# Local attention in an fp32 Trainium2 block: P divided before it is turned, and V as the stationary operand

## What is computed

```python
qkv = x @ Wqkv
q, k, v = jnp.split(qkv, 3, -1)              # then by heads: b, h, n, d
q = l2norm(q) * qs;  k = l2norm(k) * ksc
q = q * cos * scale + rotate_half(q) * sin * scale
k = k * cos * inv + rotate_half(k) * sin * inv
...
sim = jnp.einsum('bhwie,bhwje->bhwij', bq, bk2) * QK_SCALE   # 32 queries, 64 keys
sim = jnp.where(mask, -jnp.finfo(sim.dtype).max, sim)
attn = jax.nn.softmax(sim, -1)
out = jnp.einsum('bhwij,bhwje->bhwie', attn, bv2)
return out.transpose(0, 2, 1, 3).reshape(b, n, INNER) @ Wo
...
xn = (x - mu) / jnp.sqrt(var + 1e-05) * g + bln
hg = xn @ W1 + b1
a, gate = jnp.split(hg, 2, -1)
return a * jax.nn.gelu(gate, approximate=False) @ W2 + b2
```

## Time and profile before

| | us |
|---|---|
| median of three runs | 1783.48 (1780.46 to 1783.8) |
| profiled execution | 1771.68 |
| its span, first to last instruction | 1769.9 |
| TensorE busy in it | 1633.4 (92%) |
| VectorE, ScalarE, GpSimd busy | 1340.1, 1292.9, 1061.1 |

### The profile page before, as it was taken

How to read it: one execution, slowest core, us unless ns; L and a number is a source line. 1 busy time by engine, 2 the same in 40 slices (tenths; PEclk the granted TensorE clock), 3 DMA queues, 4 the chain that set the end, 5 groups by cost and what they waited for, 6 DMA issues and landing times.

```text
span 1769.9 us, 88661 instructions
## 1 busy us (share of the span) xinstructions
PE 1633.4 (92%) x36636; PEld 1264.3 (71%) x36636; DVE 1340.1 (76%) x1952; ACT 1292.9 (73%) x2124; POOL 1061.1 (60%) x767
## 2 busy tenths in 40 slices
PE   4898677799999999999999999999999999999985
PEld 2466455677777777777777777777777777777764
DVE  4465666688888878888887888888887878888852
ACT  3687445677877778777788777878777787777763
POOL 4000345567866767867678766668676676767630
PEclk8899889999999999999999999999999999999997
DMA  2000142222242222333222422222422222222220
GB/s 95 1 1 0 25 116 59 52 70 66 67 128 59 67 59 69 103 88 74 53 69 59 128 66 71 69 52 65 122 69 71 66 67 70 70 67 69 66 47 25
DMA packets 75302, 116.88 MB, mean 66 GB/s; under 512 B 17246, under 2 KB 26716, under 8 KB 74332
## 3 DMA queue, kind: packets, MB, share of 16 engines
q1 hardware_dynamic: 75228, 115.99, 26.4%
HBM read 19.04 MB, written 1.05 MB: 11 GB/s over the span
## 4 chain that ended last, share of the span: by engine, by line
PE 87%; issue 6%; ACT 4%; DVE 3%; DMA 0%; POOL 0%; ACTq 0%; SPq 0%; DVEq 0%
PE ps L684 14%; PE ps L788 10%; PE ps L671 9%; PE ps L766 9%; PE ps L731 8%; PE ps L675 7%; PE ps L674 7%; PE ps L834 4%; PE ps L724 2%; PE ps L806 2%; PE ps L808 2%; PE ps L807 2%; PE ps L801 2%; PE ps L795 2%; PE ps L582 1%
## 5 line engine op out<-in xcount | busy, mean ns | idle before, releaser
L411 POOL TENSOR_TENSOR arena<-arena,rnorm 128x1024 f32<-128x1024 f32 x192 | 361.6, 1904 | 352.3 <-ACT rnorm L1030 352.3
L402 POOL TENSOR_TENSOR arena<-arena 128x1024 f32<-128x1024 f32 x192 | 456.6, 2378 | 18.5 <-DVE arena L1349 15.1
L684 PEld LDWEIGHTS ps<-cst,arena 64*128 64x128 f32 x6144 | 224.4, 140 | 127.8 <-issue 119.0
L1345 DVE TENSOR_TENSOR arena<-ps,rope 128x1024 f32<-128x1024 f32 x192 | 234.7, 1222 | 94.9 <-issue 82.1
L684 PE MATMUL ps<-cst,arena 64*128 64x64 f32 x6144 | 276.8, 231 | 17.0 <-ACT arena L1060 9.4
L1066 ACT ACTIVATE arena<-ps 128x512 f32<-128x512 f32 x192 | 114.6, 597 | 175.5 <-PE ps L684 175.2
L1349 DVE TENSOR_TENSOR arena<-ps,rope 128x1024 f32<-128x1024 f32 x192 | 233.2, 1215 | 0.0
L674 PE MATMUL ps<-wqkv_lo,x_hi 128*128 128x512 f32 x576 | 229.2, 398 | 1.1 <-issue 1.1
L675 PE MATMUL ps<-wqkv_hi,x_hi 128*128 128x512 f32 x576 | 230.1, 399 | 0.0
L671 PE MATMUL ps<-wqkv_hi,x_lo 128*128 128x512 f32 x576 | 216.2, 457 | 14.8 <-issue 12.9
L1359 DVE TENSOR_REDUCE norm<-arena 128x16 f32<-128x1024 f32 x192 | 224.3, 1209 | 0.0
(11 more groups left out here) (120 smaller groups left out, 2824.2 us busy)
## 6 DMA issues: line engine op xcount, KB each, us to landing
v_sb<-v_nat SPq DMA_DIRECT2D x576, 130.0 KB, 2.4
v_sb<-v_nat SPq DMA_DIRECT2D x192, 65.0 KB, 2.0
wqkv_sb<-wqkv SPq DMA_DIRECT2D x6, 1536.0 KB, 6.8
v_sb<-v_sb SPq DMA_DIRECT2D x96, 65.0 KB, 2.0
wo_sb<-wo SPq DMA_DIRECT2D x6, 512.0 KB, 8.4
w_sb<-w SPq DMA_DIRECT2D x6, 341.0 KB, 7.9
x<-xT SPq DMA_DIRECT2D x1, 1024.0 KB, 6.2
out<-x SPq DMA_DIRECT2D x4, 256.0 KB, 2.3
```

Source lines behind the costliest of these rows:

```text
L402: pool.tensor_tensor(t_cos[:, m, j, :], t_cos[:, m, j, :], t_sin[:, j, :], ALU.add)\
L411: pool.tensor_tensor(x, x, rnorm[:, H * j:H * j + H].unsqueeze(2).to_broadcast([P, H, D]), ALU.mult).then_inc(s[done], 1)
L684: mm = pe.transpose(ps[0:width, bank + t, 64 * c:64 * c + 64], src[r], ident[r, r], tile_position=(64 * t, 0))
L1345: dve.tensor_tensor(t_cos[:, m, j, :].rearrange("p (h d) -> p h d", h=H), src.rearrange("p a (h d) -> p (a h) d", h=8), tc.unsqueeze(1).to ...
```

## The change

P is divided by its sum before it is turned. VectorE's `sums` adds up each row of `s_sb` (128x512 to 128x8) and takes the reciprocal; GpSimd's `normalise` multiplies `s_sb` by it, in place, 128x512 for each group of heads. `turn_p` then turns both groups in one go of 16 transposes, and `copy_p` is one copy of 128x1024. In `attend` a piece of V, 64 rows by 64 columns, stands in the array and 32 columns of P move; the output comes out by features, into banks 2 and 3, and needs no turn: `turn_o` and `o_n` are gone, and `copy_o` reads the attention's output itself. The two matmuls of a head pair go to the lower and the upper 64 partitions, so that Wo is handed over with its rows sorted by the parity of the head. `project_out` is one step. The waits follow the banks, and steps are moved: `exps` of both groups stand ahead of `gates`, the second half of `scale` behind `normalise`, `square_of(g+1, 1, 0)` ahead of `copy_p(g, 1)`, `mean` and `variance` earlier in half 1.

The core of the diff:

```diff
+            def normalise(pair, m, g):
+                n = 2 * pair + m
+                pool.wait_ge(s["recip"], CREDIT + 2 * n + g + 1)
+                p = s_sb[:, g, :, :]
+                pool.tensor_tensor(p, p, rden[:, HC * g:HC * g + HC].unsqueeze(2).to_broadcast([P, HC, SPAN]),
+                                   ALU.mult).then_inc(s["p_normed"], 1)
...
-                scale(g, 1)
+                scale(g, 1, 0)
+                scale(g, 1, 1)
+                normalise(g, 0, 0)
+                normalise(g, 0, 1)
...
-                    scale(g + 1, 0)
+                    scale(g + 1, 0, 0)
+                normalise(g, 1, 0)
+                normalise(g, 1, 1)
+                if ahead:
+                    scale(g + 1, 0, 1)
...
+            def turn_p(pair, m):
+
+                n = 2 * pair + m
+                pe.wait_ge(s["centred"], CREDIT + 2 * n + 2)
+                pe.wait_ge(s["p_normed"], CREDIT + 2 * n + 2)
...
+            def attend(pair, m, over_q=True):
+
+
+                n = 2 * pair + m
+                pe.wait_ge(s["v_moved"], CREDIT + 16 * (18 * pair + 8 + 10 * m))
+                pe.wait_ge(s["p_copied"], CREDIT + n + 1)
+                if over_q:
                     pe.wait_ge(s["roped"], CREDIT + 4 * n + 10)
                     pe.wait_ge(s["squared"], CREDIT + 2 * n + 5)
...
+                for g in range(2):
+                    for hh in range(4 * g, 4 * g + 4, 2):
+                        for w in range(4):
+                            for h, c in ((hh, 0), (hh, 1), (hh + 1, 0), (hh + 1, 1)):
+                                r = slice(D * c, D * c + D)
+                                d = D * (h % 2)
+                                at = P * (h // 2) + W * w
+                                mm = pe.matmul(ps[d:d + D, 2 + c, at:at + W],
+                                               v_sb[r, m, w, VD * h:VD * h + D], p_t[r, h, W * w:W * w + W],
+                                               start=True, stop=True, skip_group_check=True,
+                                               tile_position=(D * c, d))
+                    mm.then_inc(s["attended"], 1)
...
-            def turn_o(pair, m):
...
+            def sums(pair, m, g):
+
+                n = 2 * pair + m
+                dve.wait_ge(s["exped"], CREDIT + 2 * n + g + 1)
+                dve.wait_ge(s["p_normed"], CREDIT + 2 * n + g - 1)
+                rd = rden[:, HC * g:HC * g + HC]
+                dve.tensor_reduce(rd, s_sb[:, g, :, :], AX.X, ALU.add).then_inc(s["summed"], 1)
+                dve.wait_ge(s["summed"], CREDIT + 2 * n + g + 1)
+                dve.reciprocal(rd, rd).then_inc(s["recip"], 1)
```

More of the change, by code:

```diff
@@ L494, in _ @@
             rotate(0, 0, 1)
-            scale(0, 0)
+            scale(0, 0, 0)
+            scale(0, 0, 1)
             rotate(0, 1, 0)
@@ L770, in attend @@
-                mm.then_inc(s["attended"], 1)
-            def turn_o(pair, m):
-                n = 2 * pair + m
-                pe.wait_ge(s["o_normed"], CREDIT + 2 * n + 2)
-                pe.sem_inc(s["pe_waited"], 1)
-                for c in range(H // 2):
-                    mm = turn(2, c, o_n[:, P * c:P * c + P])
-                mm.then_inc(s["o_turned"], 1)
-            def project_out(pair, half):
-                if half == 0:
-                    pe.wait_ge(s["o_copied"], CREDIT + 2 * pair + 2)
-                    pe.wait_ge(s["w_a_loaded"], 16 * layer_of(pair) + 16)
-                    pe.wait_ge(s["centred"], CREDIT + 4 * pair + 5 if not isinstance(pair, int) or pair < SLOTS - 1
-                               else CREDIT + 4 * pair + 4)
-                for c in range(4 * half, 4 * half + 4):
+                pe.sem_inc(s["pe_waited"], 1)
@@ L860, in slot @@
                     v(g + 1, 0)
-                turn_o(g, 0)
                 scores(g, 1, 0)
@@ L866, in slot @@
                     q(g + 1, 1)
+                if out:
+                    mean(g - 1)
+                if ahead:
                     k(g + 1, 1)
-                turn_p(g, 1, 0)
                 if ff:
                     down(g - LAG)
-                turn_p(g, 1, 1)
+                turn_p(g, 1)
                 if out:
-                    mean(g - 1)
-                attend(g, 1, 0)
-                attend(g, 1, 1, over_q=ahead)
+                    variance(g - 1)
+                attend(g, 1, over_q=ahead)
                 if ahead:
@@ L1145, in slot @@
                     round_up(layer)
-                copy_p(g, 1, 0)
                 exps(g, 1, 1)
+                if out:
+                    square(g - 1)
                 if more:
                     high(g + 2, 0)
-                copy_p(g, 1, 1)
+                if ahead:
+                    square_of(g + 1, 1, 0)
+                copy_p(g, 1)
                 if after == 6:
                     round_weights(layer, 1)
-                if ahead:
-                    square_of(g + 1, 1, 0)
                 if out:
-                    square(g - 1)
+                    inverse_deviation(g - 1)
                 if ahead:
@@ L1423, in slot @@
                 centre(g, 0, 1)
+                sums(g, 0, 0)
+                sums(g, 0, 1)
                 if ahead:
@@ L1437, in slot @@
                 centre(g, 1, 1)
+                sums(g, 1, 0)
+                if out:
+                    subtract_mean(g - 1)
+                sums(g, 1, 1)
                 if ahead:
@@ L1442, in slot @@
                     add(g - LAG)
-                if out:
-                    subtract_mean(g - 1)
-                normalise(g, 1, 0)
-                normalise(g, 1, 1)
                 if ahead:
```

133 lines of the change are left out of this document (43 added, 90 removed).

## The result

The changed kernel takes 2006.38 us (median of 4 runs, 1999.82 to 2022.37) against 1781.97 us for the kernel before, run beside it: a ratio of 1.1279, 95% interval 1.1205 to 1.1352. It is slower, as forecast, but by 224 us where 94 were forecast, and the time lies well outside the range of 1826 to 1938 us. The profiled execution has a span of 2007.9 us, against 1769.9.

The account below looks back on a forecast made before the run. TensorE's queue was taken as the bound: less work but two new waits give +2.05 us per slot, 88 us over 43 slots, plus 6 in weight-split slots: +94, set on the median 1783.48 as 1878 us, range 1826 to 1938.

Parts of the forecast that it names:

- The two waits: TensorE waits 1.8 us in half 0 before `values_up`'s third tile (for `residual`), 2.4 in half 1 before attention (for `copy_p`).
- The chains: Queue order and data: half 0 ropes, `residual`, third tile at 13.1 us; half 1 sums, ropes from 6.0, square, `copy_p` 10.4.
- GpSimd's division: `normalise` of 128x512 on GpSimd: 0.97 us each, adding 3.9 to 20.5 us busy per slot.
- (c): Rival: ropes and `residual` keep up, no waits form; 1.75 us per slot saved, 1701 us; 6%, with the space around zero.
- (d): Rival: GpSimd's division at full price, 1.9 us each; +24 us on the sum, 1902 us; 10%.
- nothing is free but 0.25 us: Reading of TensorE's steady slot before the change: groups run back to back, idle only 0.25 us ahead of the second attention block.
- waits of their own: Said of the first four slots, half the clock in parts; the forecast left them and the tail as they are.
- the pair count is what stays, so I take 1.65: Attention block keeps 128 load and matmul pairs at 12.9 ns each, so 1.65 us; 0.83 to 2.3 carried into the range.
- The other bound, from the turns' tiles: Attention block's upper bound: four tiles each holding a pair 71 ns as in the turns, 18 ns per pair, 2.3 us.
- Rival (a): Attention block gets dearer: something near 2.3 us, 1939 us in all, 9%; far end 3.3 us, 2033 us, 5%.
- half 1's wait: TensorE waits 2.4 us for `copy_p`, done at 10.4; attention starts 10.5, each hand-over taken at 0.1; half 14.9 against 13.79.
- The ledger of a slot: Work -1.75 us, waits +1.8 and +2.4, less today's 0.25; +2.05 us per slot taken, +88 us over 43 slots.

Follow-up runs that it names:

- e10: Changed kernel with both TensorE waits filled by repeated work: `variance` matmul run seven times, second `values_up` tile four times over; 1934.34 us, ratio 1.0867 to the kernel before.
- e6: Kernel before with one wait added: four spare ScalarE copies ahead of the last `copy_p`, delaying half 1's attention; 1924.89 us, ratio 1.0825.
- e3: Changed kernel with attention output and turned Q swapping banks, `copy_p` ahead of the square, `residual` ahead of the second rope product; 1780.23 us, ratio 1.0005 to the kernel before.
- e5: Kernel before with rows of 64 small fp32 matmuls behind its end, varying stationary and moved columns: V 64 x P 32 2.00 us, P 32 x V 66 1.43.
- e4: Changed kernel with half 1's attention wait for `p_copied` put behind those for `roped` and `squared`; 1993.46 us, ratio 1.1213 to the kernel before.

## The prediction against the runs, step by step

**Right.** TensorE's queue is the bound and each wait counts in full. The two waits stand where they were put, with the releasers named; counted as in the forecast, from start to start less TensorE's own 0.12 and 0.35 us, they are 1.5 and 2.8 us where 1.8 and 2.4 were forecast (the views give 1.4 and 2.4, from ends that are modelled). The chains came out within 0.5 us: in half 0 the third tile at 12.64 on the slot's clock (13.1 forecast); in half 1 the rope pair from 6.08 (6.0), `copy_p` done at 10.50 (10.4), the turns at 7.22 (7.2), behind the division, as forecast. GpSimd's division took 1.04 us for 0.97, and GpSimd 24.5 us per slot for 24.4. Rivals (c) and (d) are out.

**Wrong: the clock.** The step from "nothing is free but 0.25 us" to "TensorE's queue is the bound" led to a sum in which every duration behind the waits was taken at the clock of the kernel before; the text sets no term for it. The prediction took the 1.00 of the earlier trace rows over into a kernel that waits for 4 us per slot. The runs showed in its place: some 15% of the steady stage at half clock, 70 to 83 us over 43 slots (e10), present with the old attention form as well (e6), all but gone with the waits (0.99 in e3) or with their filling (0.99 in e10). The prediction saw "half the clock in parts" and "waits of their own" in the first four slots (0.92 from 215 to 370 us of the kernel before), and didn't put the two together. It left those slots as they are; in the changed kernel that stretch runs at 0.80, and slot 4 starts 19.6 us later.

**Wrong in size: the attention block.** Taken at 1.65, measured 2.00 us at full clock in both halves, where the kernel before has 1.65 and 1.75: +0.35 and +0.25 per slot, 26 us over 43 slots. The failing step was "the pair count is what stays, so I take 1.65". The other bound, from the turns' tiles (71 ns a pair, four tiles, 18 ns), came nearer, 62 for 71 ns. What it had right is that a pair's time is that of its tile divided by the number of tiles; that a tile loaded with 64 columns took nearly what the turns' tiles take with 128 is in part luck. The runs showed in place of the pair count: a pair is set by the width of what is loaded, and the change doubled it; that it halved the number of tiles cost nothing, since four narrow ones take 1.22 us and eight 1.26. Rival (a) named the mechanism at 9%.

The rule of the Trainium skill, "TensorEngine Tiling (Array Packing)", section "Instruction Overhead", bears on this block: below some 60 columns the moved columns shouldn't matter. e5 agrees in that 16 and 32 columns take the same. But the time that the prediction made of it for this kernel, 3.3 us per block with a tile held as long as before, didn't come: 2.00.

**Wrong in size: half 1's wait.** The attention was to start at 10.5 and started at 10.98, 0.48 instead of 0.1 behind `copy_p`: the hand-over was sized by other places, not by what stood in TensorE's queue behind the wait. 0.35 to 0.38 per slot, 15 us; e4 gave 13 back.

**The ledger of a slot**: forecast +2.05; at full clock the halves are 18.1 and 15.8 us, so +3.2; of the 1.15 between, 0.60 is the block, 0.38 the order of waits, and 0.1 a slip of the sum (10.5 + 1.65 + 1.15 + 1.67 is 14.97, not 14.9, and half 1's +1.1 is +1.2); 0.1 is left unassigned. Half clock makes of +3.2 the measured +5.15 (1.9 by e10, 2.0 by the slots). Times 43: 88 forecast, and 26 + 16 + 83, and the first slots' 20, make 233 of the 238 us between the two profiled spans. The 6 us forecast for GpSimd behind the weight split aren't to be seen: the five slots take 35.3 to 36.6 us, 36.2 on the mean, like the others (36.1). There the two `scale` of half 0 start 4.1 to 4.3 us after the slot's start, as before (4.27) and not 1.9 us later, the divisions end at 9.8 to 10.0, not 11.9, and the turns wait 0.2 to 0.4.

## What to carry to other kernels

When a change puts a wait into the queue of a TensorE that was never idle, price the wait and then the clock: ask whether the work behind it will still run at full clock, and put a term for it into the sum and the range. Count small matmuls by what each tile has to load, columns times pairs over tiles, not by their number alone; here this held up to four tiles, and eight were no faster. Put the wait that is met last at the end of a list of waits, and look for the bank that lets a wait vanish before judging an idea by its first version: here the same idea was worth +12.8% and, rearranged, -0.5%.
